# A six-stage transformer kernel: the start of its MoE pass moved forward, and its weight loads merged

## The chip, the cores and the metric

One core of one Trainium2 chip. The metric is the device time of one execution in microseconds (us), the median of several runs; lower is better.

## What is computed

The reference takes x of 2 sequences x 1024 tokens x 128 features and applies six residual stages. The MoE stage is the one that the change is about (cut):

```python
x = x + 0.5 * ffn(layernorm(x)); x = x + linear_attention(layernorm(x)); x = x + 0.5 * ffn(layernorm(x))
x = x + 0.5 * moe(layernorm(x)); x = x + causal_attention(layernorm(x)); x = x + 0.5 * moe(layernorm(x))

def moe(x):                                   # 16 experts of width 64, top 2, and a shared one of width 256
    probs = softmax(x @ router_w.T)
    top_w, top_i = top_k(probs, 2); top_w = top_w / top_w.sum(-1)
    dense_w = zeros(T, 16).at[arange(T)[:, None], top_i].add(top_w)
    out = sum(dense_w[:, e, None] * ((silu(x @ Wg[e]) * (x @ Wu[e])) @ Wd[e]) for e in range(16))
    return out + sigmoid(x @ shared_gate_w) * ((silu(x @ Sg) * (x @ Su)) @ Sd)
```

## The kernel before

Everything stays on one core; x lives in SBUF. The 2048 tokens are cut into four chunks of 512 (four tiles of 128). The stages are FFN0, LIN (linear attention), FFN1, MOE0, CAUSAL, MOE1, numbered 0 to 5, and a LayerNorm is named by L = 4 x stage + chunk, so L = 12 is the first chunk of MOE0. Each engine runs its own program in a fixed order, written out by hand, and engines meet at semaphores.

The LayerNorm of a chunk is a relay: `moments` (DVE, L861 and L864), `rstd` (GpSimd, L445 on), `norm` (DVE, L876), `ln` (PE transposes L1269, then ACT's copy L620 or L623) and `split` (DVE, L889 and L890), which leaves the features as two parts, uh and ul, for matmuls of three products each (L1261 to L1263).

A feed-forward pass (`ffn`) has 16 blocks of 128 hidden units by 512 tokens: the three products, SiLU on ACT (L641), and W2 two blocks later (L1301). After a chunk's fourth W2 group DVE adds the result into x (`update`, L900). In the last chunk of FFN1, PE's order puts the `ln` of L = 12 behind block 13 and its router products (`route`, 128x18 outputs) behind block 15. DVE turns the router's output into the combine weights cw (`route` L1035 to L1043, `weigh` L1048 to L1064, with ACT's tanh between), after the norm of L = 13 and around the update of the last chunk. PE transposes cw (L1414, `weights`) after the second gate/up pair of MOE0, and ACT copies it to SBUF as cwt of 17 rows x 512 tokens: 16 experts and the shared gate.

A MoE pass (`moe`) does ten units a chunk, each of two experts (8 units, 2 x 64 hidden units) or half of the shared one (2 units). PE makes gate and up (three products each), ACT applies SiLU (L717), DVE multiplies by up (L1074) and then by the combine weight of each expert and token (L1078), and PE applies W_down two units later (L1471). For that second product the combine weights are needed with the expert on the partition axis, 64 partitions per expert. SyncE gets them there (`combine_weights`, L402 to L414): it stores cwt in a DRAM tensor of 17 rows and then reads each expert's row 64 times, broadcast over 64 partitions of the tile gb (a part of kt), two loads a unit. gb has four buffers: the load of unit m waits for the product of unit m - 4 (`hm_ready`). The store of the next chunk's weights stands in the same queue, and SyncE waits for it before it issues that chunk's loads. Everything on this path goes through the queue of SyncE.

GpSimd clears the tiles stm and kza for CAUSAL (L566, L567) in its loop at L = 14. CAUSAL isn't changed; the first tiles of its projections are made during the last units of MOE0.

## Time and profile before

| what | us |
|---|---|
| median of 3 runs | 700.85 |
| lowest and highest run | 698.91, 707.11 |
| profiled execution | 699.1 |
| its span, first to last instruction | 697.3 |
| its mean granted TensorE clock | 0.929 of full speed |

Rows of the trace are times in us from the start of the span. A busy share is that of the stretch; the DMA share is the mean over the core's 16 DMA engines.

### The profile page before, as it was taken

What the parts mean: (1) busy time and instruction counts of PE and PEld (TensorE: products, weight loads), DVE (VectorE), ACT (ScalarE), POOL (GpSimd) and SP (SyncE); (2) the same over time, 40 slices, a digit from 0 to 9 for tenths busy, and PEclk for the clock granted to TensorE, in tenths of its full rate; (3) what the DMA queues carried; (4) which work ended last, traced back from release to release, by engine and by line L of the source; (5) the groups of instructions that cost most, each with busy time, mean ns of one, the idle gap of its engine ahead of it and who ended that gap; (6) DMA issues with size and microseconds to landing.
All of it is one profiled execution on the core that took longest, in us unless ns stands there. A gap on an engine that the chain in (4) does not pass through costs nothing.

```text
span 697.3 us, 12355 instructions
## 1 busy us (share of the span) xinstructions
PE 604.0 (87%) x4284; PEld 420.7 (60%) x4284; DVE 486.7 (70%) x1526; ACT 346.3 (50%) x711; POOL 171.4 (25%) x304
## 2 busy tenths in 40 slices
PE   1876757969999987778999999998999997999998
PEld 1755546858877975544454545444544434888887
DVE  3568894657877776564788888879888521777755
ACT  3735326422232453345767767675677765332321
POOL 5574256232003361854111111202120000100000
PEclk9999989989999998556999999999999978899999
DMA  8000000022332210000000000000000001133342
GB/s 280 1 0 1 1 0 1 1 94 90 115 116 72 84 47 1 1 0 1 1 2 2 1 1 1 2 1 1 2 2 0 3 1 56 68 124 103 117 132 76
DMA packets 18669, 27.98 MB, mean 40 GB/s; under 512 B 2984, under 2 KB 7208, under 8 KB 18608
## 3 DMA queue, kind: packets, MB, share of 16 engines
q1 hardware_dynamic: 17888, 25.85, 11.5%
q10 hardware_dynamic: 720, 1.34, 0.6%
q8 instruction: 35, 0.57, 0.3%
q14 instruction: 26, 0.21, 0.1%
HBM read 25.85 MB, written 1.33 MB: 39 GB/s over the span
## 4 chain that ended last, share of the span: by engine, by line
PE 62%; DVE 14%; ACT 6%; issue 5%; POOL 3%; DMA 1%; SPq 0%; DVEq 0%; POOLq 0%
PE bank L1471 9%; PE bank L1531 9%; PE bank L1606 8%; PE bank L1574 7%; PE bank L1261 6%; PE bank L1263 6%; PE bank L1262 6%; DVE bank L1148 3%; DVE hn L876 2%; ACT arena L785 2%; DVE work L1151 2%; PE bank L1500 2%; PE bank L1512 1%; PE bank L1541 1%; PE bank L1586 1%
## 5 line engine op out<-in xcount | busy, mean ns | idle before, releaser
L785 ACT ACTIVATE arena<-bank 128x512 f32<-128x512 f32 (+3 forms) x384 | 166.3, 496 | 74.1 <-PE bank L1586 50.9
L1148 DVE CUSTOM_DVE_ANT_0 bank<-bank,mask_qk 128x512 f32<-128x512 f32 (+3 forms) x256 | 119.0, 518 | 39.4 <-PE bank L1606 39.3
L1606 PE MATMUL bank<-kza,qta 64*128 64x512 f32 (+3 forms) x384 | 138.1, 450 | 7.5 <-DVE work L1148 3.6
L1574 PE MATMUL bank<-qtb,kza 64*128 64x512 f32 (+3 forms) x384 | 134.3, 419 | 4.3 <-ACT arena L785 2.0
L1606 PEld LDWEIGHTS bank<-kza,qta 64*128 64x128 f32 x384 | 65.5, 203 | 80.9 <-DVE work L1148 43.5
L717 ACT ACTIVATE work<-bank 128x512 f32<-128x512 f32 x80 | 47.7, 597 | 119.3 <-PE bank L1263 113.3
L1151 DVE TENSOR_REDUCE work<-bank 128x1 f32<-128x512 f32 x128 | 80.2, 683 | 19.9 <-PE bank L1606 19.9
L1471 PE MATMUL bank<-dw,work 128*128 128x128 f32 x640 | 86.2, 279 | 6.7 <-DVE work L1078 6.7
L1471 PEld LDWEIGHTS bank<-dw,work 128*128 128x128 f32 x640 | 82.6, 194 | 10.9 <-issue 6.9
L1074 DVE TENSOR_TENSOR work<-work,bank 128x512 f32<-128x512 f32 x80 | 54.7, 684 | 48.2 <-PE bank L1263 42.6
L1574 PEld LDWEIGHTS bank<-qtb,kza 64*128 64x128 f32 x384 | 64.9, 191 | 31.2 <-ACT arena L785 18.4
L1531 PE MATMUL bank<-arena 128*9 128x512 f32 (+3 forms) x768 | 83.0, 505 | 0.5 <-ACT arena L785 0.4
L523 POOL CAST kza<-kt 32x512 fp32r<-32x512 f32 x48 | 29.2, 607 | 158.9 <-PE bank L1574 118.3
L445 POOL TENSOR_SCALAR rtmp<-mv 128x4 f32<-128x4 f32 x24 | 9.3, 387 | 221.1 <-DVE mv L864 220.8
L1078 DVE TENSOR_TENSOR work<-work,kt 128x512 f32<-128x512 f32 x80 | 56.2, 702 | 8.6 <-DMA kt<-cw_rows 5.9
L876 DVE TENSOR_SCALAR hn<-x,mv,rs 128x128 f32<-128x128 f32 x96 | 35.8, 436 | 20.2 <-POOL rs L462 16.5
L1586 PE MATMUL bank<-identb,mask_kq 64*128 64x64 bf16 x512 | 48.1, 198 | 0.0
L1261 PE MATMUL bank<-qta,gh 128*128 128x512 f32 x80 | 38.5, 482 | 0.0
L1269 PE MATMUL bank<-identr,hn 128*128 128x128 f32 x96 | 17.0, 305 | 24.1 <-DVE hn L876 24.1
L1301 PEld LDWEIGHTS bank<-work 128*128 128x128 f32 x256 | 33.5, 199 | 6.2 <-DVE x L900 3.0
L1301 PE MATMUL bank<-work 128*128 128x128 f32 x256 | 35.5, 285 | 2.0 <-ACT work L641 1.6
L900 DVE SCALAR_TENSOR_TENSOR x<-bank,x 128x512 f32<-128x512 f32 x24 | 16.5, 688 | 29.5 <-PE bank L1556 13.3
(179 smaller groups left out, 1078.2 us busy)
## 6 DMA issues: line engine op xcount, KB each, us to landing
kt<-cw_rows SPq DMA_DIRECT2D x160, 128.0 KB, 2.9
x<-x_in SPq DMA_DIRECT2D x4, 256.0 KB, 8.7
y_out<-x SPq DMA_DIRECT2D x4, 256.0 KB, 3.2
arena<-gw_in SPq DMA_DIRECT2D x1, 640.0 KB, 10.0
arena<-uw_in SPq DMA_DIRECT2D x1, 640.0 KB, 8.3
dw<-dw_in SPq DMA_DIRECT2D x1, 640.0 KB, 9.4
work<-q_in SPq DMA_DIRECT2D x2, 256.0 KB, 6.3
arena<-const_in ACTq DMA_DIRECT2D x1, 400.0 KB, 6.5
```

The lines of the kernel that those rows point to most:

```text
L785: act.activation(pb[:, blk % 2, h, 0:w], s_bank(n)[:, 0:w], ACT.Exp, scale=SCALE).then_inc(p_ready, 1)
L1074: link(dve.tensor_tensor(su[:, m % 2, :], sg[:, m % 2, :], bank[4 + m % 3][:, :], ALU.mult))
L1078: dve.tensor_tensor(hbuf[:, m % 3, :], su[:, m % 2, :], gb[:, m % 4, :], ALU.mult)\
L1148: ins = dve.tensor_tensor_reduce(out=src, in0=src, in1=mask_qk[:, CW - w:], scale=1.0, scalar=-3e38, op0=ALU.add, op1=ALU.max, accum_out=dst)
L1151: ins = dve.tensor_reduce(dst, src, AX.X, ALU.max)
L1261: pe.matmul(dst, ah, bl, start=start, stop=False)
L1301: ins = pe.matmul(ACC[:, t * P:(t + 1) * P], hbuf[:, m % 4, t * P:(t + 1) * P], w2[:, k, :], start=(k == 0 and t == 0), stop=(k == FB - 1) ...
L1471: ins = pe.matmul(ACC[:, t * P:(t + 1) * P], hbuf[:, m % 3, t * P:(t + 1) * P], dw[:, u, :], start=(u == 0 and t == 0), stop=(u == NU - 1) ...
L1531: ins = pe.matmul(bank[7][h * SL:h * SL + HD + 1, CW - w:CW], va[:, b, j, g * GH + h, :], pb[:, blk % 2, h, 0:w], start=(j == 0), stop=Tru ...
L1574: ins = pe.matmul(s_bank(n)[:, 0:w], kz(s, h, j // CT)[pair(h), j % CT * P:(j % CT + 1) * P], qtb[pair(h), s % 2, (c + 1) * CW - w:(c + 1) ...
L1586: ins = pe.matmul(s_bank(n)[:, a * 2 * SL:(a + 1) * 2 * SL], mask_kq[r, a, :], identb[r, r], start=False, stop=True, skip_group_check=True)
L1606: pe.matmul(a_bank(n)[:, 0:w], qta[pair(h), slot(b, g), i * P:(i + 1) * P], kz(s, h, half)[pair(h), 0:w], start=True, stop=True).then_inc( ...
```

## The change

FFN1's tail is put in another order on all three engines: the `ln` of L = 12 after block 11, the router after block 13, the transpose of cw before the last W2 group. DVE takes the moments of L = 12, 13 and 14 before the updates and computes cw before the last update. The clears of stm and kza move to the opening, half of kza to DVE. The two loads of a unit become one: the source is a view of two rows, each repeated 64 times by a zero step, and the destination is gb's 128 partitions; for the shared units it is one row, repeated 128 times. The semaphore count that DVE waits for is halved. The whole diff:

```diff
--- before.py
+++ after.py
@@ -408,10 +408,11 @@
                     m = NU * r + u
                     if m >= 4:
                         sp.wait_ge(hm_ready, m - 3)
-                    for a in range(2):
-                        e = 2 * u + a if u < E_ // 2 else E_
-                        sp.dma_start(gb[a * FE:(a + 1) * FE, m % 4, :], cw_rows[r, e:e + 1, :].to_broadcast([FE, CW]))\
-                            .then_inc(gb_loaded[m % 4], 16)
+                    if u < E_ // 2:
+                        rows_of = cw_rows[r, 2 * u:2 * u + 2, :].unsqueeze(1).to_broadcast([2, FE, CW])
+                    else:
+                        rows_of = cw_rows[r, E_:E_ + 1, :].to_broadcast([P, CW])
+                    sp.dma_start(gb[:, m % 4, :], rows_of).then_inc(gb_loaded[m % 4], 16)
 
             def store(c):
                 sp.wait_ge(x_ready, 4 * MOE1 + c + 1)
@@ -525,6 +526,8 @@
                     pool.wait_ge(kz_ready[s], n + h + 1)
 
             pool.memset(nhalf[:, :], -0.5)
+            pool.memset(stm[:, :, :, :, :].bitcast(F32), 0.0)
+            pool.memset(kza[:, 0:2, :, :].bitcast(F32), 0.0)
             rstd(0)
             pool.wait_ge(small_loaded, 32)
             pool.tensor_scalar(b2q[:, :], rows[:, R_B2:R_B2 + D], 0.25, None, ALU.mult)
@@ -561,10 +564,6 @@
                     rstd(L)
                     if L <= 12:
                         xadd(L - 1)
-                if L == 14:
-
-                    pool.memset(stm[:, :, :, :, :].bitcast(F32), 0.0)
-                    pool.memset(kza[:, :, :, :].bitcast(F32), 0.0)
             for i in range(TB):
                 tile(0, i)
                 if i % 2 == 0:
@@ -641,8 +640,12 @@
                     act.activation(hbuf[:, m % 4, :], bank[1 + m % 4][:, :], ACT.Silu,
                                    bias=small[:, S_B1 + k:S_B1 + k + 1],
                                    scale=small[:, S_S1 + k:S_S1 + k + 1]).then_inc(h_ready, 1)
-                    if k == 1:
+                    if k == 1 and m < 28:
                         ln(4 * p + n // FB + 1)
+                    if m == 27:
+                        ln(4 * MOE0)
+                    if m == 30:
+                        route(0)
                     if k == 2 and n // FB < NC - 1:
                         residual(4 * p + n // FB + 1)
                     if p == FFN0 and k == 3:
@@ -653,7 +656,7 @@
                         if n // FB == 1:
                             act.activation(vh[:, :], raw_u, ACT.Copy).then_inc(hi_ready, 1)
                 if p == FFN1:
-                    route(0)
+                    weights(0)
 
             def features(dst_r, dst_e, src):
 
@@ -704,8 +707,6 @@
 
             def moe(p):
                 r0 = 4 if p == MOE1 else 0
-                if p == MOE0:
-                    weights(r0)
                 for n in range(NC * NU):
                     c, u = divmod(n, NU)
                     m = n + (NC * NU if p == MOE1 else 0)
@@ -903,14 +904,20 @@
             def ffn(p):
                 for c in range(NC):
                     L = 4 * p + c
-                    split(L + 1)
+                    if L + 1 < 4 * MOE0:
+                        split(L + 1)
                     norm(L + 2)
+                    if L >= 9 and L < 11:
+                        moments(L + 3)
+                    if L + 2 == 4 * MOE0:
+                        split(L + 2)
                     if L + 1 == 4 * MOE0:
                         route(0)
+                        weigh(0)
+                        moments(L + 3)
                     update(L, 0.25)
-                    if L + 1 == 4 * MOE0:
-                        weigh(0)
-                    moments(L + 3)
+                    if L < 9:
+                        moments(L + 3)
                     if p == FFN0 and c in (1, 2):
 
                         hi, lo, raw = ((gh, gl, raw_g), (vh, vl, raw_u))[c - 1]
@@ -1074,7 +1081,7 @@
                     link(dve.tensor_tensor(su[:, m % 2, :], sg[:, m % 2, :], bank[4 + m % 3][:, :], ALU.mult))
                     if m >= 3:
                         dve.wait_ge(down_done, 2 * NC * FB + m - 2)
-                    dve.wait_ge(gb_loaded[m % 4], 32 * (m // 4 + 1))
+                    dve.wait_ge(gb_loaded[m % 4], 16 * (m // 4 + 1))
                     dve.tensor_tensor(hbuf[:, m % 3, :], su[:, m % 2, :], gb[:, m % 4, :], ALU.mult)\
                         .then_inc(hm_ready, 1)
                     if u == 1 and c > 0:
@@ -1226,6 +1233,7 @@
 
 
             moments(0)
+            dve.memset(kza[:, 2:4, :, :].bitcast(F32), 0.0)
             dve.wait_ge(q_loaded, 32)
             dve.tensor_scalar(w1f[:, :], raw_q[:, 0, :], -128.0, None, ALU.add).then_inc(w1_ready, 1)
             dve.wait_ge(w1_hi, 1)
@@ -1287,10 +1295,14 @@
                         f = slice(k * P, (k + 1) * P)
                         mm3(bank[1 + m % 4][:, :], w1h[:, f], w1l[:, f], uh[:, tok(c)], ul[:, tok(c)])\
                             .then_inc(y_full, 1)
-                        if k == 1:
+                        if k == 1 and m < 28:
                             ln(4 * p + c + 1)
-                        if n == NC * FB - 1 and p == FFN1:
+                        if m == 27:
+                            ln(4 * MOE0)
+                        if m == 29:
                             route(4 * MOE0, 0)
+                    if n == NC * FB + 1 and p == FFN1:
+                        weights(0)
                     if n >= 2:
                         c, k = divmod(n - 2, FB)
                         m = n - 2 + (16 if p == FFN1 else 0)
@@ -1441,8 +1453,6 @@
 
                 gate_up(0)
                 gate_up(1)
-                if p == MOE0:
-                    weights(r0)
                 gate_up(2)
                 for n in range(NC * NU + 2):
                     if n < NC * NU:
```

The queue of SyncE, where the chunks of the first MoE pass follow the initial loads. dw is W_down, cwt the transposed weights, kt the tile that holds gb. Before:

```order
L396 DMA arena<-gw_in 128x1280
L397 DMA arena<-uw_in 128x1280
L398 DMA dw<-dw_in 128x1280
L402 DMA cw_rows<-cwt 17x512
L413 DMA kt<-cw_rows 64x512 x20
```

And now:

```order
L397 DMA arena<-uw_in 128x1280
L398 DMA dw<-dw_in 128x1280
L402 DMA cw_rows<-cwt 17x512
L415 DMA kt<-cw_rows 128x1x512 x8
L415 DMA kt<-cw_rows 128x512 x2
```

Twenty loads a chunk are now ten, eight of them of the form with two source rows; the store stands where it stood.

PE at the end of FFN1 and the start of MOE0, from the last router products (128x18) on. work is the hidden block that W2 takes, late is W1, gh and vh are the gate and up weights. Before:

```order
L1263 MATMUL bank<-kt,wh 128x18
L1301 MATMUL bank<-work 128x128 x12
L1261 MATMUL bank<-qta,gh 128x512
L1262 MATMUL bank<-kt,gl 128x512
L1263 MATMUL bank<-kt,gh 128x512
```

And now:

```order
L1271 MATMUL bank<-wh,kt 128x18
L1313 MATMUL bank<-work 128x128 x4
L1269 MATMUL bank<-qta,late 128x512
L1270 MATMUL bank<-kt,late 128x512
L1271 MATMUL bank<-kt,late 128x512
L1313 MATMUL bank<-work 128x128 x4
L1269 MATMUL bank<-qta,late 128x512
L1270 MATMUL bank<-kt,late 128x512
L1271 MATMUL bank<-kt,late 128x512
L1313 MATMUL bank<-work 128x128 x8
L1426 MATMUL bank<-identr,cw 17x128 x4
L1313 MATMUL bank<-work 128x128 x4
```

The router is now followed by two more W1 blocks, and the transpose of cw stands ahead of the last W2 group, where it stood behind two gate/up pairs.

DVE at the same place, from the update of the third chunk or the moments behind it. x<-bank,x is the update, hn the norm, lg to dd the router's part, cw its last result. Before:

```order
L900 SCALAR_TENSOR_TENSOR x<-bank,x 128x512
L861 BN_STATS stats<-x 128x6 x4
L864 BN_AGGR mv<-stats 128x2 x4
L889 CAST kt<-ft 128x512
L890 TENSOR_TENSOR qta<-ft,kt 128x512
L876 TENSOR_SCALAR hn<-x,mv,rs 128x128 x4
L1035 COPY dd<-bank 128x4
L1036 COPY lg<-bank 128x72
L1039 MAX m<-lg 128x8 x4
L1042 MAX_INDEX ix<-m,lg 128x8 x4
L1043 TENSOR_TENSOR dd<-m 128x4
L900 SCALAR_TENSOR_TENSOR x<-bank,x 128x512
```

And now:

```order
L862 BN_STATS stats<-x 128x6 x4
L865 BN_AGGR mv<-stats 128x2 x4
L890 CAST kt<-ft 128x512
L891 TENSOR_TENSOR qta<-ft,kt 128x512
L901 SCALAR_TENSOR_TENSOR x<-bank,x 128x512
L877 TENSOR_SCALAR hn<-x,mv,rs 128x128 x4
L1042 COPY dd<-bank 128x4
L1043 COPY lg<-bank 128x72
L1046 MAX m<-lg 128x8 x4
L1049 MAX_INDEX ix<-m,lg 128x8 x4
L1050 TENSOR_TENSOR dd<-m 128x4
L1055 CAST ixf<-ix 128x8
```

The moments and the split now stand ahead of the third chunk's update, and the first instruction of `weigh` follows the router's part directly, ahead of the last update.

## Rows read from the trace of the kernel before

**Rows 1.** The page: busy us of each engine; the queue of SyncE's copies

```profile
PE 604.0 (87%) x4284; PEld 420.7 (60%) x4284; DVE 486.7 (70%) x1526; ACT 346.3 (50%) x711; POOL 171.4 (25%) x304
...
q1 hardware_dynamic: 17888, 25.85, 11.5%
```

**Rows 2.** Stretches: us, busy PE PEld DVE ACT POOL, clock, DMA share, GB/s

```profile
145.50:146.50 1.00, 0.00 (x0) 0.00 (x0) 0.00 (x0) 0.41 (x1) 1.00 (x2) 1.00 0.07 25
148.00:151.50 3.50, 0.00 (x0) 0.00 (x0) 0.37 (x1) 0.00 (x0) 1.31 (x1) 0.70 0.57 174
151.00:152.25 1.25, 0.28 (x1) 0.32 (x2) 1.12 (x2) 0.34 (x1) 0.00 (x0) 0.50 0.55 207
156.00:207.00 51.00, 50.43 (x322) 44.57 (x320) 40.87 (x122) 14.74 (x26) 4.94 (x7) 1.00 0.34 106
207.00:265.00 58.00, 51.90 (x327) 45.08 (x328) 41.64 (x112) 27.47 (x49) 23.88 (x43) 0.97 0.20 65
603.00:691.00 88.00, 87.66 (x554) 77.54 (x555) 63.84 (x168) 24.73 (x44) 1.26 (x2) 1.00 0.35 113
282.00:326.00 44.00, 34.67 (x144) 21.56 (x143) 23.47 (x75) 20.93 (x36) 29.18 (x65) 0.50 0.00 1
```

**Rows 3.** Waits of the whole span: us in total, times, longest us

```profile
PE bank L1471 <- DVE work L1078: 6.7, 1, 6.7
...
DVE work L1078 <- DMA kt<-cw_rows: 5.9, 1, 5.9
```

**Rows 4.** The chain of waits at the start of MOE0: start us, us, what

```profile
143.49 0.60 ACT cwt L703
...
144.10 2.83 DMA cw_rows<-cwt
...
146.95 0.51 SPq L413
...
147.50 3.53 DMA kt<-cw_rows
```

**Rows 5.** Timeline of PE, end of FFN1: start us, us, instruction [idle before]

```profile
131.40 0.66 PE L1269 MATMUL bank<-identr,hn 128*128 128x128 f32 x4 [0.21 <-DVE hn L876]
...
135.97 0.28 PE L1261 MATMUL bank<-wl,kt 128*128 128x18 f32 x1 [0.37 <-DVE qta L890]
```

**Rows 6.** Timeline of DVE, end of FFN1

```profile
125.42 0.69 DVE L900 SCALAR_TENSOR_TENSOR x<-bank,x 128x512 f32<-128x512 f32 x1 [2.92 <-PE bank L1301]
...
137.88 0.15 DVE L1035 COPY dd<-bank 128x4 f32<-128x4 f32 x1
...
139.24 0.14 DVE L1043 TENSOR_TENSOR dd<-m 128x4 f32<-128x4 f32 x1
...
140.90 0.16 DVE L1048 CAST ixf<-ix 128x8 f32<-128x8 uint32 x1
...
142.10 0.22 DVE L1064 TENSOR_TENSOR cw<-oh 128x64 f32<-128x64 f32 x1
```

**Rows 7.** Timelines of GpSimd and DVE at the opening, and of GpSimd in MOE0

```profile
5.28 0.23 POOL L445 TENSOR_SCALAR rtmp<-mv 128x4 f32<-128x4 f32 x1 [4.46 <-DVE mv L864]
...
8.84 0.43 DVE L1230 TENSOR_SCALAR work<-work 128x512 f32<-128x512 int32 x1 [3.65 <-DMA work<-q_in]
...
144.91 0.95 POOL L566 MEMSET stm<- 128x1024 f32 x1
145.80 3.51 POOL L567 MEMSET kza<- 128x4096 f32 x1
```

**Rows 8.** Timeline of DVE: products with the combine weights, late in both passes

```profile
239.46 0.69 DVE L1078 TENSOR_TENSOR work<-work,kt 128x512 f32<-128x512 f32 x1
...
265.17 0.69 DVE L1078 TENSOR_TENSOR work<-work,kt 128x512 f32<-128x512 f32 x1
...
689.64 0.69 DVE L1078 TENSOR_TENSOR work<-work,kt 128x512 f32<-128x512 f32 x1
...
691.92 0.69 DVE L1078 TENSOR_TENSOR work<-work,kt 128x512 f32<-128x512 f32 x1
```

**Rows 9.** Timeline of SyncE's queue: the first loads of MOE1

```profile
586.74 13.45 SPq L413 DMA_DIRECT2D kt<-cw_rows  x11
```

## The prediction

> **What bounds the kernel now.** I read the page's busy shares and DMA rows first, then the waits, the chain around the start of the first MoE pass (MOE0), the busy time by stretch, and the timelines of PE, DVE and SyncE there. PE is busy 87% of the span, and the DMA engines are nearly idle: the queue of the weight loads uses 11.5% of 16 engines [rows 1]. In the plain MoE stretches PE is full (87.66 of 88.00 us in 603 to 691) [rows 2], with one unit in 2.28 us (two last products of DVE, 689.64 and 691.92) [rows 8]. The combine weights arrive in time for 79 of 80 products. The one exception is the first: DVE waits 5.9 us for a load and PE 6.7 us for DVE [rows 3]. Its chain is serial: ACT's copy of the weights at 143.49, the store to DRAM 2.83 us, the first issue of a load at 146.95, the landing of the second at 147.50 + 3.53 = 151.03 [rows 4].
>
> **The clears.** The GpSimd clears take 0.95 and 3.51 us, beside the idle stretch of PE [rows 7], and nobody waits for them; taking them away gives nothing. At the opening GpSimd idles for 4.46 us up to 5.28; 0.95 and half of 3.51 (1.76) fit. The half on DVE comes at 5.19, ahead of an idle time of 3.65 us that a load ends at 8.84 [rows 7]. No row shows a wide memset on DVE: at GpSimd's speed it takes 1.76 us, by the DVE row of 0.43 us for 512 columns 4 x 0.43 = 1.7. Both fit in 3.65. It could at worst hold up the GpSimd chain that runs beside it (5.28 onwards) by its own length. Value 0, bounds 0 and +1.8 us.
>
> **The moves.** Before, PE's router products (135.97) stand behind the last W1 block; then come three W2 groups and two gate/up pairs before the transpose of the weights. I replay the end of FFN1 with the same durations. The statistics of the first MoE chunk no longer wait for the residual update at 125.42 [rows 6], so its norm on DVE ends at about 128.2 (PE's transposes of it stood at 131.40 [rows 5]). PE now wants them at 127.9 and waits 0.3 us. The feature copy follows at 129.9, the split at 131.1, and PE reaches the router at 131.9, finishing at 133.4. DVE first does the update (134.8) and the norm of chunk 13 (135.8), then the router part (1.5 us, from 137.88 to 139.38 before) to 137.3, ACT's tanh to 137.5, the weights (before 140.90 to 142.32, so 1.4) to 138.9 [rows 6]. PE is at its transpose at 138.0 and waits 0.9 us. The copy starts at 139.4 instead of 143.49: **4.1 us earlier**. The first gate/up product stays at about 140.0, since the waits of 0.3 and 0.9 us replace others of 0.21, 0.37 and some small ones. The PE gap then shrinks from 6.7 to about 3 us. Loads that land as fast as before would give -4.1 us (bounds -2 and -6: a late link in the replay, or a clock that no longer falls in the gap, as it did at 149.3 to 0.50 for 4 us of work).
>
> **The loads.** This is the term that decides. An expert unit's load was two copies with 64 outer rows, all read from one DRAM row; it becomes one copy whose source is 2 rows, each read 64 times, and whose destination has 128 rows. The bytes (256 KB) stay and one issue of some 0.55 us goes. The question is over how many DMA engines such a copy is spread. The trace has two kinds. The store of the weights has 17 rows: while it alone moves, the DMA share is 0.07 (one engine of 16 is 0.0625) at 25 GB/s, so it runs on **one engine**. The loads with 64 rows reach 0.55 to 0.57 at 174 and 207 GB/s [rows 2], so on many. 17 has no divisor up to 16 but 1; 64 has 16. A copy appears to be divided evenly by its outer count, and the source's outer count is now 2: two engines, 128 KB on each. The Trainium skill, page "DMA: Bandwidth & Descriptors", section "Why a DMA increments its semaphore by 16 and not by 1", says it outright: the number of engines is the largest up to 16 that divides the slowest dimension of both sides. By that rule the loads take two engines and the sum below stands, and where it doesn't hold for such a copy rival A's time does; the store's row (one engine for 17 rows) agrees with it, and no row here shows a copy whose two sides differ.
>
> Rate of one engine: 25 GB/s alone; 207/(0.55 x 16) = 23.5 for these loads at 151.00; 106/(0.34 x 16) = 19.5 and 113/(0.35 x 16) = 20.2 in the steady stretches [rows 2]. I take 23.5, the row of the same loads with a backlog: 131,072 B / 23.5 = **5.58 us for an expert unit**; ends 5.24 and 6.72. Four buffers keep three more loads queued, so latency hides but throughput doesn't, and 5.58 is more than PE's 2.28 (4.56 at half clock). Per chunk of ten units: 8 x 5.58 = 44.6 us. Between chunks the two shared units (128 rows, all engines, 16 KB each per engine: 1.4), the store behind them (34 KB on one engine: 1.4), its landing (0.3) and 1.05 from the next issue (146.95) to the first bytes (148.00) make 4.15.
>
> First pass: issue 146.95 - 4.1 = 142.85, bytes from 143.9, the 32nd expert load done at 143.9 + 178.6 + 3 x 4.15 + 0.3 = 335.2, then DVE's last three products, 0.7 + 2 x 1.37 = 3.4: 338.6. Before, that product ended at 265.86 [rows 8]: +72.7. Second pass: its loads start at 586.74 [rows 9], now 659.4, so bytes from 660.5; + 178.6 + 12.4 + 0.3 + 3.4 = 855.2, against 692.61: **+162.6**. What follows (W_down, update, store) is unchanged. Span 697.3 + 162.6 = 859.9. The profiled execution took 699.1, 1.8 more than its span, which gives 861.7; the median of the three runs is 1.75 above that execution, so 863. In 207 to 265 PE is busy 51.90 of 58 us at nearly full clock [rows 2]; one unit there takes 3.7 us (seven from 239.46 to 265.17 [rows 8]), so 3.3 us of PE and 6.6 at half clock. If the clock falls there, up to 16 units x 1 us come on top.
>
> **Rivals.**
> A, the loads stay on 16 engines (the destination's 128 rows decide, or the copy is cut otherwise). For: a load of 256 KB in 128 rows is ordinary, and every 64-row load spread. Against: the store on one engine. Then loads have slack (2.28 us a unit, four buffers), and only the moves count: 700.85 - 4.1 = 697, not slower than before. It decides from an engine count of 5 upwards, where 256 KB take less than 2.28 us.
> B, two engines, but at the pace of the steady rows, 19.5 GB/s: 6.72 us a unit, 64 x 1.14 = 73 more, 936. For: those rows are long and the same kind of load. Against: there 16 engines pull at once, and packets of a lone pair should disturb each other less, as in the store's 25.
> C, lone-engine pace: 5.24 us, 64 x 0.34 = 22 less, 841.
>
> **Chances.** Two engines 0.82, of which my value and C together 0.64 and B (with the half clock in the first pass) 0.18; A 0.15; 0.03 that the loads spread and the opening or the earlier waits cost more than the moves give. A measurement tells about 1% from no change, 7 us. Under A the 4 us stay within 1% mostly, with the clock's stretch at 0.50 in 282 to 326 [rows 2] able to move it either way. So faster 0.05, same 0.13, slower 0.82. The range reaches from C with shorter gaps (six of 4.15 us, less most of them, 820) to B with some half clock (955); A lies outside with its 0.15.
>
> **What would show it.** Right: DMA share in the MoE stretches near 0.125 at some 47 GB/s, expert loads landing 15 to 20 us after issue, DVE waiting for loads at nearly every unit (some 3 us each), products 5.6 us apart, the two shared units close behind, PE mostly idle at 1.2 GHz. The move is right if the copy of the weights starts at 139 to 140. Wrong: landings of 3 to 4 us and a share of 0.35 as before. Wrong in size: products spaced by 5.2 or 6.7, or more than 5 us between chunks. A norm(0) on DVE later than 10.6 would charge the clears.

## The result, and the profile after

The changed kernel took 863.79 us (median of 4 runs, 859.32 to 867.14), the kernel before 703.98 on the same chip: a ratio of 1.230 (95% interval 1.223 to 1.238). The profiled execution took 861.5 us, with a span of 859.7. Among many executions of one kernel some run at a lower granted clock and take one to three per cent longer; the medians have them in, the ratios leave them out.

The page first: busy times, the queue of SyncE's copies, and the shares of the chain that ended last.

```profile
PE 671.4 (78%) x4284; PEld 464.1 (54%) x4284; DVE 484.8 (56%) x1527; ACT 346.7 (40%) x711; POOL 167.9 (20%) x304
...
q1 hardware_dynamic: 15712, 25.84, 8.5%
...
DMA 40%; PE 31%; DVE 11%; ACT 4%; issue 3%; POOL 2%; SPq 1%; DVEq 0%; POOLq 0%
```

The engines have the same number of instructions as before, but for one more on DVE (its half of the clears), and the queue moves the same bytes (25.84 MB, 25.85 before). Its share of 16 engines' span fell from 11.5% to 8.5% [rows 1] while the kernel got slower: a resource can look idler on the page and be the bound. The chain says where the time is: 40% of the span is DMA.

The waits of the whole span (engine, line and what it waited for: us in total, times, longest), answering to [rows 3]:

```profile
DVE work L1085 <- DMA kt<-cw_rows: 192.4, 57, 8.1
ACT work L718 <- DVE work L1085: 120.0, 32, 5.9
```

One wait of 5.9 us on a load became 57 waits with 192.4 us. ACT's silu waits behind DVE, and PE behind both.

Busy time by stretch (us, busy PE PEld DVE ACT POOL with counts, clock, DMA share, GB/s), answering to [rows 2]:

```profile
148.00:150.00 2.00, 0.00 (x0) 0.00 (x0) 0.00 (x0) 0.00 (x0) 0.00 (x0) 1.00 0.13 49
150.00:188.00 38.00, 25.52 (x114) 20.56 (x114) 14.83 (x52) 4.86 (x9) 3.64 (x5) 0.78 0.17 63
352.00:407.00 55.00, 44.13 (x195) 27.50 (x195) 26.92 (x87) 24.72 (x45) 30.25 (x66) 0.50 0.00 1
665.00:850.00 185.00, 132.03 (x658) 108.24 (x656) 67.88 (x184) 31.79 (x60) 2.53 (x4) 0.80 0.18 62
```

The first row is the plainest: only expert loads are moving, and the share is 0.13, which is 2 of 16 engines (0.125), at 49 GB/s, so 24.5 GB/s an engine. The longer stretches have the shared units' loads and the store in them as well. The clock of 0.78 and 0.80 is a mean over parts at full and parts at half speed. PE is busy only 25.52 of the 38 us there; with the loads fast again (next section) it is busy 36.80 of them, and the clock is 1.00.

The timeline of DVE in the first chunk of MOE0 (start us, us, instruction, idle before it and what ended that): the products with the combine weights.

```profile
172.76 0.69 DVE L1085 TENSOR_TENSOR work<-work,kt 128x512 f32<-128x512 f32 x1 [1.26 <-DMA kt<-cw_rows]
177.96 0.69 DVE L1085 TENSOR_TENSOR work<-work,kt 128x512 f32<-128x512 f32 x1 [2.56 <-DMA kt<-cw_rows]
183.19 0.69 DVE L1085 TENSOR_TENSOR work<-work,kt 128x512 f32<-128x512 f32 x1 [3.94 <-DMA kt<-cw_rows]
188.27 0.69 DVE L1085 TENSOR_TENSOR work<-work,kt 128x512 f32<-128x512 f32 x1 [3.79 <-DMA kt<-cw_rows]
189.59 0.69 DVE L1085 TENSOR_TENSOR work<-work,kt 128x512 f32<-128x512 f32 x1
190.92 0.69 DVE L1085 TENSOR_TENSOR work<-work,kt 128x512 f32<-128x512 f32 x1
197.66 0.69 DVE L1085 TENSOR_TENSOR work<-work,kt 128x512 f32<-128x512 f32 x1 [5.32 <-DMA kt<-cw_rows]
```

Expert units stand 5.08 to 5.23 us apart, each ended by a load; in [rows 8] it was 2.28 (689.64 to 691.92; those two are shared units, but the expert units of that chunk stood 2.27 to 2.45 apart as well). The two shared units (189.59, 190.92), whose loads repeat one row 128 times, follow at 1.33 us. Then comes a hole up to the next chunk's first unit: 9.39 us from 188.27 to 197.66, 4.3 more than a unit.

SyncE's queue shows what that hole is made of (start us, us, instruction):

```profile
140.93 0.31 SPq L402 DMA_DIRECT2D cw_rows<-cwt  x1
143.78 36.51 SPq L415 DMA_DIRECT2D kt<-cw_rows  x10
180.33 0.29 SPq L402 DMA_DIRECT2D cw_rows<-cwt  x1
189.98 14.60 SPq L415 DMA_DIRECT2D kt<-cw_rows  x5
```

The store issued at 180.33 lets the next load out only at 189.98: 9.65 us, where at 140.93, with nothing queued ahead, it took 2.85. Most of the 9.65 is the last expert load of the old chunk, whose product comes at 188.27; the next load goes out 1.7 us after it. Then that load lands alone, 7.68 us from 189.98 to 197.66. The very first load shows the same 7.68 (143.78 to 151.46).

What moves meanwhile (columns as in the stretches above):

```profile
180.50:183.00 2.50, 0.90 (x4) 0.38 (x3) 0.00 (x0) 0.00 (x0) 0.00 (x0) 1.00 0.68 225
183.50:188.00 4.50, 4.07 (x14) 2.96 (x14) 0.98 (x2) 0.60 (x1) 0.00 (x0) 0.62 0.13 51
```

When the store is issued, the loads of two expert units (products at 183.19 and 188.27) are unfinished, and the second shared load has just been issued. That one goes over the other engines at once (share 0.68); from 183.5 on only two engines work (0.13), and the store isn't done before they are.

The moved code at the end of FFN1, on PE and DVE (two timelines), answering to [rows 5] and [rows 6]:

```profile
128.72 0.66 PE L1277 MATMUL bank<-identr,hn 128*128 128x128 f32 x4 [0.21 <-DVE hn L877]
...
139.66 0.61 PE L1426 MATMUL bank<-identr,cw 128*17 128x128 f32 x4 [0.45 <-DVE cw L1071]
...
152.30 2.05 PE L1481 MATMUL bank<-dw,work 128*128 128x128 f32 x8 [6.58 <-DVE work L1085]
```

```profile
134.83 0.69 DVE L901 SCALAR_TENSOR_TENSOR x<-bank,x 128x512 f32<-128x512 f32 x1 [3.11 <-PE bank L1313]
...
139.39 0.22 DVE L1071 TENSOR_TENSOR cw<-oh 128x64 f32<-128x64 f32 x1
...
151.46 0.69 DVE L1085 TENSOR_TENSOR work<-work,kt 128x512 f32<-128x512 f32 x1 [8.11 <-DMA kt<-cw_rows]
```

The weights are ready 2.7 us earlier (139.39 against 142.10), and the store goes out 3.2 earlier (140.93 against 144.10). Nothing is left of it at the first product: 151.46 against the 151.13 before, because the slow landing took it back. PE's gap there is 6.58 us, as long as the 6.7 of [rows 3].

### The profile page after: what moved, and what is told of

Same layout as the page of the kernel before. It is cut to its first block, busy times and chain, and to the rows that moved or that the text cites. A ratio compares the mean times of both kernels' runs of the same rounds, so it can differ in the third digit from the quotient of the medians.

```text
span 859.7 us, 12276 instructions
## 1 busy us (share of the span) xinstructions
PE 671.4 (78%) x4284; PEld 464.1 (54%) x4284; DVE 484.8 (56%) x1527; ACT 346.7 (40%) x711; POOL 167.9 (20%) x304
## 3 DMA queue, kind: packets, MB, share of 16 engines
q1 hardware_dynamic: 15712, 25.84, 8.5%
HBM read 25.85 MB, written 1.33 MB: 32 GB/s over the span
## 4 chain that ended last, share of the span: by engine, by line
DMA 40%; PE 31%; DVE 11%; ACT 4%; issue 3%; POOL 2%; SPq 1%; DVEq 0%; POOLq 0%
DMA kt<-cw_rows 37%; PE bank L1541 8%; PE bank L1616 6%; PE bank L1584 6%; DMA cw_rows<-cwt 3%; DVE bank L1155 2%; ACT arena L786 2%; DVE hn L877 1%; PE bank L1510 1%; DVE work L1158 1%; PE bank L1522 1%; PE bank L1481 1%; PE bank L1269 1%; PE bank L1551 1%; PE bank L1596 1%
## 5 line engine op out<-in xcount | busy, mean ns | idle before, releaser
L1481 PE MATMUL bank<-dw,work 128*128 128x128 f32 x640 | 109.5, 327 | 77.2 <-DVE work L1085 39.9
L1085 DVE TENSOR_TENSOR work<-work,kt 128x512 f32<-128x512 f32 x80 | 56.0, 700 | 196.6 <-DMA kt<-cw_rows 192.4
L1481 PEld LDWEIGHTS bank<-dw,work 128*128 128x128 f32 x640 | 100.1, 234 | 92.4 <-DVE work L1085 43.8
L1616 PE MATMUL bank<-kza,qta 64*128 64x512 f32 (+3 forms) x384 | 140.9, 457 | 8.0 <-DVE work L1155 4.2
L718 ACT ACTIVATE work<-bank 128x512 f32<-128x512 f32 x80 | 47.7, 597 | 233.9 <-DVE work L1085 120.0
L1584 PE MATMUL bank<-qtb,kza 64*128 64x512 f32 (+3 forms) x384 | 138.0, 431 | 4.3 <-ACT arena L786 2.1
L1541 PE MATMUL bank<-arena 128*9 128x512 f32 (+3 forms) x768 | 87.0, 527 | 0.5 <-ACT arena L786 0.4
L1584 PEld LDWEIGHTS bank<-qtb,kza 64*128 64x128 f32 x384 | 66.9, 197 | 32.8 <-ACT arena L786 19.6
L1081 DVE TENSOR_TENSOR work<-work,bank 128x512 f32<-128x512 f32 x80 | 54.6, 682 | 17.7 <-PE bank L1271 17.3
L1277 PE MATMUL bank<-identr,hn 128*128 128x128 f32 x96 | 19.1, 334 | 33.2 <-DVE hn L877 33.2
L1269 PE MATMUL bank<-qta,gh 128*128 128x512 f32 x80 | 44.6, 558 | 0.0
L877 DVE TENSOR_SCALAR hn<-x,mv,rs 128x128 f32<-128x128 f32 x96 | 33.4, 413 | 18.4 <-POOL rs L463 16.5
L1270 PE MATMUL bank<-kt,gl 128*128 128x512 f32 x80 | 36.9, 462 | 0.0
```

The source lines that it names most:

```text
L1081: link(dve.tensor_tensor(su[:, m % 2, :], sg[:, m % 2, :], bank[4 + m % 3][:, :], ALU.mult))
L1085: dve.tensor_tensor(hbuf[:, m % 3, :], su[:, m % 2, :], gb[:, m % 4, :], ALU.mult)\
L1269: pe.matmul(dst, ah, bl, start=start, stop=False)
L1481: ins = pe.matmul(ACC[:, t * P:(t + 1) * P], hbuf[:, m % 3, t * P:(t + 1) * P], dw[:, u, :], start=(u == 0 and t == 0), stop=(u == NU - 1) ...
L1541: ins = pe.matmul(bank[7][h * SL:h * SL + HD + 1, CW - w:CW], va[:, b, j, g * GH + h, :], pb[:, blk % 2, h, 0:w], start=(j == 0), stop=Tru ...
L1584: ins = pe.matmul(s_bank(n)[:, 0:w], kz(s, h, j // CT)[pair(h), j % CT * P:(j % CT + 1) * P], qtb[pair(h), s % 2, (c + 1) * CW - w:(c + 1) ...
```

## The experiments

Two theories stood against each other. **T**: the number of DMA engines that a copy goes over is the largest one up to 16 that divides the outer counts of both its sides; the merged load's source has 2, and this is the whole loss. Rivals: one load of 256 KB from two rows is slow however it is written (R3), any source with nested loops is slow (R4), or the moves and clears carry part of the loss (R1, R2).

### Two loads per unit put back

```diff
-                    if u < E_ // 2:
-                        rows_of = cw_rows[r, 2 * u:2 * u + 2, :].unsqueeze(1).to_broadcast([2, FE, CW])
-                    else:
-                        rows_of = cw_rows[r, E_:E_ + 1, :].to_broadcast([P, CW])
-                    sp.dma_start(gb[:, m % 4, :], rows_of).then_inc(gb_loaded[m % 4], 16)
+                    for a in range(2):
+                        e = 2 * u + a if u < E_ // 2 else E_
+                        sp.dma_start(gb[a * FE:(a + 1) * FE, m % 4, :], cw_rows[r, e:e + 1, :].to_broadcast([FE, CW]))\
+                            .then_inc(gb_loaded[m % 4], 16)
```

> The changed kernel with the kernel before's two loads per unit (64 outer rows each, one DRAM row as source); moves and clears as in the changed kernel. Theory T (the whole loss is the merged load, which falls onto two DMA engines because its source has 2 outer rows): 701 us, within 1% of the kernel before (700 to 704 there); the ACT copy of the weights still starts at about 140.3 us, the first load is issued at about 143.8 and lands in 3.5 to 4 us instead of 7.6, so MOE0 starts some 3 us earlier; the DMA share in the MoE stretches is back at 0.34 or more. Rival R1 (the moves or the clears cost time of their own, hidden in the changed kernel behind the slow loads): over 707 us, with FFN1's tail or the opening longer than before. Rival R2 (most of the +160 us is the moves, not the load): over 780 us.

Measured: 701.89 us (12 runs), ratio 0.998 (0.994 to 1.002). The whole +160 us is gone with this one edit; R2 falls, and so does R1's loss from the moves. The stretch 150 to 188:

```profile
150.00:188.00 38.00, 36.80 (x236) 32.25 (x236) 32.86 (x108) 10.45 (x19) 4.93 (x7) 1.00 0.35 114
```

PE is busy 36.80 of 38 us where it was 25.52, at full clock, and the share is 0.35. The first product and PE after it:

```profile
148.01 0.69 DVE L1084 TENSOR_TENSOR work<-work,kt 128x512 f32<-128x512 f32 x1 [3.94 <-DMA kt<-cw_rows]
148.84 1.13 PE L1480 MATMUL bank<-dw,work 128*128 128x128 f32 x8 [2.38 <-DVE work L1084]
```

It comes at 148.01, 3.50 us after the first load's issue at 144.51 and 3.1 earlier than before. PE's gap shrank to 2.38 us.

### The merged load alone

The diff is the load's part of the change, on the kernel before.

> The kernel before with the merged load alone; order and clears as before. Theory T: 866 to 868 us, that is the changed kernel's 863.8 plus the 2 to 4 us by which its moves start MOE0's first load earlier; units 5.13 to 5.2 us apart, DMA share about 0.17 in the MoE stretches. Rival R1 or R2 (the moves or clears carry a share of the loss): clearly under 860 us, by that share.

Measured: 862.29 us (2 runs), ratio 1.227 (1.215 to 1.239); the first load goes out at 148.85, lands 7.7 us later, and the waits are the same:

```profile
DVE work L1079 <- DMA kt<-cw_rows: 194.4, 59, 9.4
```

With the run before it this closes the question of which part: the load alone gives the loss, without it there is none. The 2 to 4 us that the moves should have saved on top (866 to 868 expected) don't show in the time of two runs whose interval is 2.4% wide. They show in the trace. Counted from the same mark, PE's transposes of the norm before (124.90 here, 123.06 in the changed kernel), the first product of MOE0 stands 31.65 us later here and 28.40 in the changed kernel, and the end of the last one 216.3 and 213.6: the moves keep some 3 us to the end of MOE0.

### The same merged load with its loops swapped

```diff
-                        rows_of = cw_rows[r, 2 * u:2 * u + 2, :].unsqueeze(1).to_broadcast([2, FE, CW])
+                        rows_of = cw_rows[r, 2 * u:2 * u + 2, :].unsqueeze(0).to_broadcast([FE, 2, CW])
...
-        return cat([w.transpose(1, 0, 2).reshape(D, -1), shared], 1)
+        return cat([w.reshape(E_ // 2, 2, D, FE).transpose(2, 0, 3, 1).reshape(D, -1), shared], 1)
...
-        "dw_in": blocks(cat([v[m + "Wd"].reshape(-1, D), v[m + "Sd"]], 0)),
+        "dw_in": blocks(cat([v[m + "Wd"].reshape(E_ // 2, 2, FE, D).transpose(0, 2, 1, 3).reshape(-1, D), v[m + "Sd"]], 0)),
```

The source is now read as 64 steps of (row 2u, row 2u + 1), so partition p gets the weights of expert 2u + p mod 2. The host lays the experts' hidden columns out to match.

> The changed kernel with its one load per expert unit, but with the source's loops swapped: 64 outer steps that stay on the same place, 2 rows inside them, to 128 rows of the destination; the hidden columns of an expert pair are interleaved on the host so that row p belongs to expert 2u + p mod 2. Same 256 KB in 128 destination rows, one issue, same two DRAM rows read. Theory T (the engine count follows the outer counts of both sides, 64 and 128 here): spread over 16 engines, DMA share over 0.3 and above 100 GB/s in the MoE stretches, units 2.3 us apart, 697 to 703 us in all, 0 to 3 us below the kernel with two loads. Rival R3 (a single load of 256 KB into 128 rows from two rows is itself slow, whatever the order of its loops): stays at about 860 us, units 5.1 us apart, DMA share 0.13 to 0.18.

Measured: 702.65 us (12 runs), ratio 0.995 (0.989 to 1.000).

```profile
150.00:188.00 38.00, 36.76 (x237) 32.58 (x237) 31.97 (x106) 10.46 (x19) 4.93 (x7) 1.00 0.32 104
```

```profile
145.88 0.69 DVE L1085 TENSOR_TENSOR work<-work,kt 128x512 f32<-128x512 f32 x1 [3.43 <-DMA kt<-cw_rows]
...
679.62 0.69 DVE L1085 TENSOR_TENSOR work<-work,kt 128x512 f32<-128x512 f32 x1
681.90 0.69 DVE L1085 TENSOR_TENSOR work<-work,kt 128x512 f32<-128x512 f32 x1
```

This is the run that tells most: the same two rows, the same 256 KB into the same 128 partitions, one DMA and one issue, and only the order of the source's loops differs. It lands 2.98 us after its issue (142.90 to 145.88) where the changed kernel's takes 7.68, and expert units of the last chunk (679.62, 681.90) are 2.28 apart. R3 falls. That one issue less per unit saves something (0 to 3 us were expected) isn't shown: 702.65 against 701.89.

### Four, eight and two outer steps

Two loads of 64 rows per unit, each from one row as in the kernel before, with the source written as k outer steps (here 4 of 16):

```diff
+                        sp.dma_start(gb[a * FE:(a + 1) * FE, m % 4, :],
+                                     cw_rows[r, e:e + 1, :].unsqueeze(0).to_broadcast([4, 16, CW]))\
+                            .then_inc(gb_loaded[m % 4], 16)
```

> The changed kernel with two loads of 64 rows per unit, each with its source written as 4 outer steps on the same row of 16 inner ones. Same bytes, same destination as in the kernel before. Theory T: 4 engines; at the changed kernel's rate of about 25.5 GB/s per engine (131,072 B in 5.13 us) 256 KB take 2.57 us, against 2.28 to 2.31 of PE: about 0.3 us more for each of 64 expert units, some 15 to 30 us more than the kernel with two plain loads, so 715 to 735 us; DMA share up to 0.25 in the MoE stretches. Rival R3 (what makes the load slow is that it is one DMA of two rows): as the kernel with two plain loads, 701 us. Rival R4 (any source whose loops aren't a plain repeat of one row is slow): 860 us or more.

> Two loads of 64 rows per unit, source written as 8 outer steps on the same row of 8 inner ones. Theory T: 8 engines; by the rate seen with 4 (units 2.59 us apart) 256 KB need 1.3 us, below PE's 2.28, so 701 to 705 us, DMA share over 0.3. Rival R4 (nested source loops are slow as such, 4 outer steps by chance less than 2): well over 705 us.

> Two loads of 64 rows per unit, each from one row as in the kernel before, source written as 2 outer steps of 32. Theory T: 2 engines, as the changed kernel, units 5.1 to 5.2 us apart, 860 to 870 us. Rival R3 (the merging into one DMA from two rows makes it slow): 701 us. If the two DMAs of a unit land on different pairs of engines instead, units 2.6 us apart and about 737 us, as with 4 outer steps.

Measured, with the stretch 150 to 188 of each (2, 4, then 8 steps, one fence each):

```profile
150.00:188.00 38.00, 22.83 (x109) 18.83 (x110) 14.82 (x52) 4.87 (x9) 3.64 (x5) 0.77 0.13 51
```

```profile
150.00:188.00 38.00, 29.54 (x170) 25.92 (x171) 24.74 (x67) 7.85 (x14) 3.65 (x5) 0.86 0.24 90
```

```profile
150.00:188.00 38.00, 37.66 (x239) 33.26 (x238) 32.87 (x108) 10.49 (x19) 4.95 (x7) 0.98 0.34 116
```

| outer steps of the source | us, median (runs) | ratio (95% interval) | DMA share, GB/s in 150 to 188 | expert units apart where loads end the wait, us | packets of q1 on the page |
|---|---|---|---|---|---|
| 2 | 927.16 (2) | 1.317 (1.308 to 1.326) | 0.13, 51 | 5.17 | 15648 |
| 4 | 737.03 (2) | 1.049 (1.039 to 1.059) | 0.24, 90 | 2.58 | 15968 |
| 8 | 700.02 (10) | 0.995 (0.991 to 0.999) | 0.34, 116 | hardly a wait, PE's 2.28 | 16608 |
| 64 (two plain loads) | 701.89 (12) | 0.998 (0.994 to 1.002) | 0.35, 114 | a wait for the first only, PE's 2.28 | 17888 |

Two of my expectations were off in size. With 4 steps the time came 2 us above the upper end. With 2 steps it came at 927 and not 860 to 870. The timeline of DVE says why:

```profile
186.05 0.69 DVE L1085 TENSOR_TENSOR work<-work,kt 128x512 f32<-128x512 f32 x1 [3.87 <-DMA kt<-cw_rows]
191.22 0.69 DVE L1085 TENSOR_TENSOR work<-work,kt 128x512 f32<-128x512 f32 x1 [3.88 <-DMA kt<-cw_rows]
196.38 0.69 DVE L1085 TENSOR_TENSOR work<-work,kt 128x512 f32<-128x512 f32 x1 [3.87 <-DMA kt<-cw_rows]
201.53 0.69 DVE L1085 TENSOR_TENSOR work<-work,kt 128x512 f32<-128x512 f32 x1 [3.86 <-DMA kt<-cw_rows]
```

The last two are the shared units. I had written their sources in 2 steps as well, and they take 5.15 each in place of 1.33: 16 x 3.8 = 61 us. A run was made to check this, with the shared units' loads plain again.

> Two loads of 64 rows with 2 outer source steps for the expert units, but the shared units' loads as in the kernel before. Settles why the version with 2 outer steps everywhere took 927 us and not 863: its expert units were 5.15 us apart as in the changed kernel, but the shared units too, which there are 1.33 apart; 16 of them, 16 x 3.8 = 61 us. Expected: 863 to 868 us, shared units 1.3 us apart. If single-row sources are slower in themselves: above 900 us.

Measured: 879.62 us (2 runs), ratio 1.250 (1.240 to 1.259). The shared units are back at 1.3 us apart (192.45, 193.77), and 47.5 us went, where 61 were expected. This form stays 15.8 us above the changed kernel. A chunk of MOE0 takes 47.7 to 48.1 us from first load to first load where the changed kernel takes 46.0 to 46.2: about 1.8 us a chunk. Two places show in the timelines. The first load of a chunk lands 8.48 to 8.93 us after its issue in MOE0, and not 7.68 (once 8.32); and the seventh expert product comes 5.9 to 6.4 us after the sixth, where it was 5.2 to 5.4. Why two copies take longer there than one stays open.

### The clears alone

```diff
+            pool.memset(stm[:, :, :, :, :].bitcast(F32), 0.0)
+            pool.memset(kza[:, 0:2, :, :].bitcast(F32), 0.0)
...
-                if L == 14:
-
-                    pool.memset(stm[:, :, :, :, :].bitcast(F32), 0.0)
-                    pool.memset(kza[:, :, :, :].bitcast(F32), 0.0)
...
+            dve.memset(kza[:, 2:4, :, :].bitcast(F32), 0.0)
```

> The kernel before with its clears moved to the opening alone. Predicted value 0, bounds 0 and +1.8 us: time within 1% of the kernel before; the norm of the first chunk on DVE at 10.6 to 10.9 us, where it was 10.58; the DVE clear (2048 fp32 columns) takes about 1.76 us and the load of the quantised weights still ends what DVE waits for at about 9 us. If the half of the changed kernel's lateness of 0.3 to 0.5 us in the feed-forward comes from the clears, it is here too.

Measured: 703.77 us (11 runs), ratio 0.996 (0.992 to 1.001). DVE at the opening:

```profile
5.53 1.76 DVE L1227 MEMSET kza<- 128x2048 f32 x1 [0.38 <-issue]
9.05 0.43 DVE L1229 TENSOR_SCALAR work<-work 128x512 f32<-128x512 int32 x1 [1.76 <-DMA work<-q_in]
...
10.94 1.10 DVE L874 TENSOR_SCALAR hn<-x,mv,rs 128x128 f32<-128x128 f32 x4
```

The clear takes 1.76 us and ends 1.76 before DVE goes on with the load that it waits for anyway. The norm stands at 10.94, 0.36 later than before (10.58), which could be put down to the clears. The other runs say no: the norm stands at 10.77 with the clears moved and two plain loads, and at 11.34 in a kernel that leaves the clears where they were (the split store alone, below). What varies is when that load lands: 8.84 to 9.57 over the runs.

### The store split into 16 rows and one

The prediction rested on the store of 17 rows running on one engine. If so, 16 rows of it should spread.

```diff
-                sp.dma_start(cw_rows[r], cwt[:, r % 2, :]).then_inc(cw_stored, 16)
-                sp.wait_ge(cw_stored, 16 * (r + 1))
+                sp.dma_start(cw_rows[r, 0:E_, :], cwt[0:E_, r % 2, :]).then_inc(cw_stored, 16)
+                sp.dma_start(cw_rows[r, E_:NR, :], cwt[E_:NR, r % 2, :]).then_inc(cw_stored, 16)
+                sp.wait_ge(cw_stored, 32 * (r + 1))
```

On the kernel with the loops swapped (two sets of runs), on the kernel before, and on the changed kernel:

> The kernel of the load with 64 outer steps (moves and clears as in the changed kernel) with the store of the combine weights split: 16 rows in one DMA, the 17th in another, in place of 17 rows in one. Theory T (engines by the outer count): the 16 rows spread over 16 engines and only 2 KB stay on one, so the store sheds up to 34,816 B / 25 GB/s = 1.4 us, less one more issue of 0.1 to 0.4; store issue to first load 1.9 to 2.2 us where it is 2.83 to 2.87 now. The first products of both MoE passes come about 1 us earlier: 700 to 702 us. Rival R5 (the store is all fixed cost; its size or its engines count for nothing): still 2.8 us or more, time unchanged or up to 1 us longer.

> The kernel with the split store, the merged load of 64 outer steps and the moves once more, on another occasion, to narrow its interval and to have a profile whose stretch at half clock behind MOE0 is short. Expected from the parts: 3.1 us for the moves and 2 x 1.25 for the store (issue to first load 1.59 and 1.58 us at the starts of MOE0 and MOE1, where it was 2.84): 5.6 us, 0.8%, so a ratio of 0.992, 697 to 699 us where the kernel before has 704. Rival R6 (the first run was luck, the parts are worth nothing): ratio 0.997 to 1.00.

> The kernel before with the store split into 16 rows and one row, nothing else. Theory T: first load of MOE0 at about 145.7 us where it was 146.95, the same at MOE1, 2.5 us in all: 701 to 702 us against 704, ratio 0.9965. If the cover is gone elsewhere (the two more issues per chunk on SP delay a load that is waited for): no gain.

> The changed kernel with the store split. Its time between chunks (from a chunk's last expert unit to the next one's first 9.4 to 11.1 us, so 4.2 to 5.9 beyond a unit) was explained by the store of 34 KB on one engine behind the queued loads. With 16 rows on 16 engines 1.2 us of each gap go: 8 x 1.2 = 10 us, 852 to 856 us; the unit period stays 5.13 to 5.2. If the gap is only the draining of the loads that are queued ahead: unchanged, 860 to 866.

SyncE's queue in the first of them:

```profile
141.58 0.34 SPq L402 DMA_DIRECT2D cw_rows<-cwt  x1
141.96 0.33 SPq L403 DMA_DIRECT2D cw_rows<-cwt  x1
143.17 17.53 SPq L416 DMA_DIRECT2D kt<-cw_rows  x10
```

From the store's issue to the first load are 1.59 us, against 2.85 (144.10 to 146.95 in [rows 4]), in spite of one more issue, and better than the 1.9 to 2.2 expected; R5 falls. 32 KB at the 25 GB/s of one engine [rows 2] are 1.3 us, and 1.26 went. The page's queue q1 has 128 packets more (16736 for 16608): in each of the 8 stores 16 engines and one, where it was one.

On the whole time a gain isn't shown. With the loops swapped the ratio is 0.989 (0.985 to 0.994) on the first occasion and 0.996 (0.990 to 1.002) on the second, where the parts add up to 0.992; the second leaves R6 standing. On the kernel before it is 0.997 (0.993 to 1.0005), as expected and not told apart from 1. The 0.989 rests on five of twelve runs, and the medians of all runs say nothing of the kind: 703.87 against 704.2 for the kernel before on the same occasion, 704.14 against 703.43, and on the kernel before 704.04 against 703.43, where 697 to 702 had been expected. What is shown is the shorter path from the store to the load, not a shorter kernel.

On the changed kernel: 855.67 us (2 runs), 8.1 less than its 863.79, where 10 were expected; the ratios, 1.216 (1.207 to 1.224) and 1.230 (1.223 to 1.238), just touch. From a store's issue to the next load it takes 9.39 to 9.64 us in the middle of the passes, where it was 9.65 to 10.58: a mean gain of 0.7 us, not the 1.2 expected. So the store's one engine is a small part of the hole between chunks; most of it is the draining of the expert loads queued ahead and then a landing with nothing behind it.

## Why the prediction was right, point by point

The forecast was 863.0, the median 863.79, and the mechanism is shown: the merge alone gives the loss, its undoing or the swapped loops take it away, and the number of outer steps sets its size. But the match to 1 us is luck: its terms were off by up to 27 us and cancelled. In the profiled execution the span is 859.7 as forecast (859.9), and its pieces are not: issue of the first load 143.78 for 142.85 (+0.9); MOE0 from there to the end of its last product 192.9 for 195.8 (-2.9); from there to MOE1's first load 331.3 for 320.8 (+10.5); MOE1 187.1 for 195.8 (-8.7).

- **Two engines.** Right. Share 0.13 with only expert loads moving, a packet count that fits 2 engines exactly, and a dose that scales. Of the signs named, the share, DVE's wait at nearly every unit (192.4 us in 57, 3.4 each) and the close shared units came. PE was not mostly idle, though: it is busy 25.52 of the 38 us in 150 to 188.
- **The rate.** Mis-sized. I took 23.5 GB/s from the 16-engine rows with a backlog and had the store's 25 as an end (rival C's). Measured 25.4: 5.16 us a unit and not 5.58, so 64 x 0.42 = 27 us too much. That is rival C's pace, whose time was 841, and by the prediction's own sign (products 5.2 apart) it was wrong in size. The row nearest in kind was the store, a transfer with few engines at work, and I weighed it against the other for no shown reason.
- **Between chunks.** I had 4.15 us beyond a unit; it is 4.3 to 5.9 (9.39, 10.20, 10.65 in MOE0, 10.18, 11.06, 9.90 in MOE1, less 5.13), in all 5.7 us more. I added the store's 1.4 us and 1.35 for issue, first bytes and landing. A lone landing costs 7.68 - 5.16 = 2.5 beyond its bytes.
- **The end of MOE0.** I let the last product end 3.4 us after the last expert load. There the tail is PE's again: from the last expert unit's product at 325.93 to the end at 336.64 are 10.7 us, with 7.67 between the last two products. The kernel before had the same tail, 10.3 us from 255.55 to 265.86, and the forecast should have carried it over: some 7 us too little. In MOE1 the 3.4 were right (851.68 to 855.02). The clock's fall that I had priced at up to 16 us shows in this tail (granted 0.66 in 330 to 337); before it, units ended by a load stay 5.1 us apart, so it cost nothing there.
- **Not foreseen: +10.5 us between the passes.** The stretch at half clock was 352 to 407 and longer, where it had been 282 to 326. I first took it for a result of the loads. The other runs take that away: from the last product's start to MOE1's store it is 318.7 us before and 329.2 after, but 316.6 (8 outer steps), 317.8 and 321.2 with the plain and the swapped loads, 320.4 and 320.9 with two kernels that load as slowly as the changed one (2 outer steps everywhere, the merge alone), and 332.0 and 329.2 in executions of two that load fast (clears alone, split store alone), which took 716.6 and 712.4 us in all. So slow loads don't bring it by themselves. It spreads over some 16 us, from 316.6 to 332.7, over the profiled executions; what sets it stays open. Without these 10.5 us the span would have been 849, an estimate, and the forecast 11 us too high.
- **The moves.** Right in kind, close in size. Measured from one mark, PE's transposes of the norm before (122.56 before, 123.06 after), the copy of the weights starts 20.93 us later before and 17.25 after: 3.7 us gained, for 4.1. Over all runs it is 20.5 to 20.9 with the old order (4 kernels) and 16.0 to 17.3 with the new (10). With fast loads the PE gap fell from 6.7 to 2.38 us, for about 3. Under the slow loads some 3 us of it reach the end of MOE0, as the merge alone shows; against the kernel before, the landing of the first load, 3.5 us longer, hides it. The copy of the weights starts at 140.31, just outside the 139 to 140 named as the sign. On the whole time the gain isn't shown: two ratios of 0.995 have intervals that end at 0.999 and 1.000, but the clears alone gave 0.996.
- **The clears.** 0, as said. The DVE clear took 1.76 us, as both estimates had it.
- **Rival A** is what the change would have been with an outer count of 8 or more: five kernels with the moves and fast loads (two of them with the split store) gave ratios of 0.998, 0.995, 0.995, 0.989 and 0.996, with 0.995 worked out (0.992 for those two). The clears alone, worth nothing, gave 0.996 too, and the medians of all runs lie between 4.2 us below the kernel before on the same occasion and 0.7 above. So these runs bear out that nothing is lost, and don't measure the 4 us.

## What to carry to other kernels

Before two copies are merged into one, write down the outer count of each side: it sets how many DMA engines work, and a broadcast written as (2 rows, 64 repeats) or (64 repeats, 2 rows) moves the same bytes at 49 or over 100 GB/s. Then compare the time of one load on that many engines with the time its buffer gives it. A queue share on the page that falls while waits on that queue rise is the sign of it, and the page's packet count, which here changed by exactly one packet per copy and engine, tells how many engines each copy used.

Move work ahead of a transfer only after looking at the transfer itself: here 3.7 us gained ahead of it were offset by one landing that took 3.5 longer.

## What the runs showed of the hardware that was not expected

- One DMA engine moves some 25 GB/s in 2 KB rows whether 1, 2 or 4 of them work: 25 GB/s at a share of 0.07 [rows 2], 5.17 us for 128 KB with 2, 2.58 us for 64 KB with 4. With all 16 called on it was 19.5 to 23.5 [rows 2].
- A store with nothing ahead of it let its successor go 2.85 us after the issue, and 1.59 with 16 of its 17 rows on 16 engines. Behind two unfinished expert loads on two engines it took 9.65 to 10.58, though 14 engines were idle for most of that (share 0.13 in 183.5 to 188). A later copy that can use the other engines goes ahead meanwhile (share 0.68 in 180.5 to 183). Copies of one queue that share an engine wait for each other there.
- Two copies of 64 rows in 2 steps land 0.6 to 1.2 us later than one of 128 rows with the same bytes per engine (8.48 to 8.93 in MOE0 against 7.68, once 8.32); the second is issued 0.66 us after the first.
